# Two-layer graph kernel: the last Gaussian's square is moved ahead of the logarithm, a quarter of it to GpSimd, and four smaller edits beside it

## The reference

```python
# layer 0: four Gaussians of each adj element, normalised over the four, summed along the row
w  = exp(-0.5 * (adj[..., None] - mean) ** 2 / (1e-14 + prec ** 2))   # (8, 1024, 1024, 4)
ws = sum(w / sum(w, -1), axis=2)                                      # (8, 1024, 4)
h  = concat over k of ws[..., k] * (x @ W0[k].T)                      # (8, 1024, 512)
x1 = layernorm(x + h)
# layer 1: one of four experts for each batch, then batch norm over the batches of an expert
top1 = argmax(mean(x1, rows) @ router_w + router_b)
out  = adj @ (x1 @ expert_w[top1])
y    = relu(batchnorm_per_expert(out) * gamma + beta)
return layernorm(x1 + y)
```

## Time and profile before

| what | value |
|---|---|
| time, median of 3 runs | 885.05 us (884.5 to 885.08) |
| the profiled execution's own time | 887.86 us |
| its span | 886.1 us |
| busy share of the span PE / DVE / ACT / POOL | 85% / 85% / 87% / 78% |
| solo exponential of tile 0, tile 63 starts at | 16.9 us, 717.2 us |

### The profile page before, as it was taken

One profiled execution on the slowest core, in us unless ns is written; L12 is line 12 of the kernel. 1 busy time (PEld: TensorE's weight loads), 2 busy tenths in 40 slices (PEclk: granted clock), 3 DMA queues, 4 the chain that ended last, 5 costly groups with the idle time before them and its releaser, 6 DMA issues.

```text
span 886.1 us, 12505 instructions
## 1 busy us (share of the span) xinstructions
PE 753.0 (85%) x3922; PEld 349.8 (39%) x3922; DVE 755.4 (85%) x1643; ACT 766.9 (87%) x774; POOL 687.7 (78%) x772
## 2 busy tenths in 40 slices
PE   1444469799999999999999999999999999997661
PEld 1111124344444444444444444444444444445440
DVE  2999988699999999999999999999999992227994
ACT  6999998799999999999999999999999961116983
POOL 6699999988888888888888888888888622004794
PEclk9966679999999999999999999999999999998996
DMA  8799886977797779778977797779787728229999
GB/s 231 210 270 261 190 238 166 225 183 192 193 240 193 193 192 239 193 192 195 242 193 190 196 240 192 193 182 249 191 190 168 153 86 330 95 83 392 348 383 359
DMA packets 263925, 191.71 MB, mean 216 GB/s; under 512 B 210098, under 2 KB 210098, under 8 KB 262322
## 3 DMA queue, kind: packets, MB, share of 16 engines
q1 hardware_dynamic: 263714, 190.90, 79.7%
q10 hardware_dynamic: 144, 0.00, 0.0%
HBM read 91.78 MB, written 48.76 MB: 159 GB/s over the span
## 4 chain that ended last, share of the span: by engine, by line
ACT 35%; DVE 26%; POOL 19%; PE 12%; issue 4%; DMA 2%; SPq 0%; POOLq 0%; DVEq 0%; ACTq 0%
DVE ps_t L967 19%; ACT wgt L654 12%; PE ps_z L1136 6%; ACT ps_t L663 6%; ACT ps_t L665 5%; ACT adj_in L648 5%; ACT ps_t L659 5%; POOL adj_cut L512 3%; DVE x_in L951 3%; PE ps_o L1154 3%; DVE wgt L929 3%; POOL x_turn L523 2%; POOL adj_in L507 2%; PE ps_t L1154 2%; POOL adj_cut L510 2%
## 5 line engine op out<-in xcount | busy, mean ns | idle before, releaser
L1136 PE MATMUL ps_z<-adjT,x1p 128*128 128x512 f16 x1536 | 341.3, 379 | 0.0
L1122 PE MATMUL ps_h<-w0T,x_turn 128*128 128x512 f16 x768 | 194.4, 407 | 74.8 <-DVE x_in L951 65.0
L967 DVE TENSOR_TENSOR ps_t<-ps_t,wgt 128x1024 f32<-128x1024 f32 x192 | 234.9, 1224 | 19.0 <-ACT ps_t L659 17.8
L929 DVE SCALAR_TENSOR_TENSOR wgt<-wgt,ps_t 128x1024 f32<-128x1024 f32 x192 | 224.7, 1214 | 15.8 <-ACT ps_t L665 15.8
L1136 PEld LDWEIGHTS ps_z<-adjT,x1p 128*128 128x128 f16 x1536 | 150.2, 98 | 180.5
L648 ACT ACTIVATE wgt<-adj_in,neg_mu 128x1024 f32<-128x1024 f32 x192 | 205.6, 1134 | 7.5 <-POOL neg_mu L567 7.4
L654 ACT ACTIVATE wgt<-wgt 128x3072 f32<-128x3072 f32 x64 | 176.5, 2757 | 0.0
L1154 PE MATMUL ps_o<-zT,w_sel 128*128 128x512 f16 x696 | 161.2, 382 | 4.9 <-DMA w_sel<-w_planes 4.1
L1122 PEld LDWEIGHTS ps_h<-w0T,x_turn 128*128 128x128 f16 x768 | 74.9, 103 | 184.7 <-issue 107.1
L512 POOL TENSOR_TENSOR adj_cut<-adj_in,adj_cut 128x1024 f16<-128x1024 f32 x64 | 136.6, 2134 | 5.3
L1154 PEld LDWEIGHTS ps_o<-zT,w_sel 128*128 128x128 f16 x696 | 68.3, 98 | 88.2 <-DMA w_sel<-w_planes 4.6
(11 more groups left out here) (221 smaller groups left out, 778.2 us busy)
## 6 DMA issues: line engine op xcount, KB each, us to landing
adj_in<-in_adj_dram SPq DMA_DIRECT2D x64, 512.0 KB, 4.0
x_in<-in_x_dram SPq DMA_DIRECT2D x64, 256.0 KB, 4.3
x_spill<-x_in SPq DMA_DIRECT2D x28, 512.0 KB, 3.4
out_spill<-o_stage SPq DMA_DIRECT2D x50, 256.0 KB, 3.1
w_sel<-w_planes SPq DMA_DIRECT2D x8, 1024.0 KB, 8.0
adjT<-x_spill SPq DMA_DIRECT2D x6, 1024.0 KB, 10.2
out_dram<-adjT SPq DMA_DIRECT2D x5, 1024.0 KB, 7.8
adjT<-out_spill SPq DMA_DIRECT2D x4, 1024.0 KB, 12.5
```

Source lines behind the costliest of these rows:

```text
L929: v.scalar_tensor_tensor(out=wgt[:, m % 2, j, :], in0=wgt[:, m % 2, j, :], scalar=SUM_SCALE / W0_SCALE, in1=tot, op0=ALU.mult, op1=ALU.mul ...
L967: v.tensor_tensor(tot, tot, wgt[:, n % 2, j, :], ALU.add).then_inc(dve_tot, 1)
L1122: last = te.matmul(ps_h[:, n % 2, :], xT[:, n % 2, left, c, :], w0T[:, right, c, :], start=(c + i == 0), stop=(c == C - 1 and i == 2))
L1136: last = te.matmul(ps_z[:, u % 2, :], x1p[:, b % 2, left, t, k * P:(k + 1) * P], adjT[:, b % 2, right, t, half * HALF:(half + 1) * HALF], ...
```

## The change

What it does:

1. ACT's square for the solo Gaussian goes from its place behind the others' exponential to one ahead of the logarithm of the tile before (`square(n, SOLO, ...)` ahead of `sum_reciprocal(n - 1)`).
2. From tile 9 (`SQ_FROM`) ACT squares only columns 256 to 1023 of it. POOL does columns 0 to 255 with a multiply-add and a multiply, in place, after its two cuts; it waits for ACT's three other squares of that tile, and the solo exponential waits for POOL (`pool_sq`).
3. x is no longer multiplied by 16 (`X_SCALE`) ahead of its cut: one POOL instruction a tile less.
4. DVE makes its three adds onto `tot` one behind the other; `weighted` for kernels 2 and 3 comes behind them.
5. SP's fetch of a batch's expert weights is written one iteration earlier; its waits go with it (`dve_route`, `pe_o`).
6. In iteration 12 alone, where two z units are to be taken, the second is taken behind the others' exponential, and its low part one iteration later.

```diff
@@ sync, iteration n
-                if u % T == 0 and 0 <= u < TILES:
-                    m = u // T
+                if (u + 1) % T == 0 and 0 <= u + 1 < TILES:
+                    m = (u + 1) // T
...
                     sp.wait_ge(dve_route, m + 1)
-                    wait(sp, pe_o, u)
+                    wait(sp, pe_o, u + 1)
@@ gpsimd
-                g.tensor_scalar(tile, tile, X_SCALE, 1.0, ALU.mult, ALU.mult).then_inc(pool_xs, 1)
-                pool.wait_ge(pool_xs, m + 1)
...
+            def square(m):
+                cols = adj_in[:, m % ADJ_RING, 0:POOL_SQ]
+                pool.wait_ge(act_sq, NK * m + NK - 1)
+                g.tensor_scalar(cols, cols, spread_of[:, SOLO:SOLO + 1], neg_mu[:, SOLO:SOLO + 1],
+                                ALU.mult, ALU.add).then_inc(pool_line, 1)
+                pool.wait_ge(pool_line, m - SQ_FROM + 1)
+                g.tensor_tensor(cols, cols, cols, ALU.mult).then_inc(pool_sq, 1)
...
                     cut_x(n + 2)
+                if SQ_FROM <= n < TILES:
+                    square(n)
@@ scalar
                 act.wait_ge(act_sq, NK * n + NK)
+                wait(act, pool_sq, n - SQ_FROM + 1)
                 wait(act, dve_ws, NK * n - 1)
...
+                if n < TILES:
+                    act.wait_ge(pool_al, n + 1)
+                    if n == 0:
+                        load_spread(SOLO)
+                    first = POOL_SQ if n >= SQ_FROM else 0
+                    if first:
+                        act.wait_ge(act_sq, NK * n + NK - 1)
+                    square(n, SOLO, adj_in[:, n % ADJ_RING, first:NR], first)
                 if 0 <= n - 1 < TILES:
                     sum_reciprocal(n - 1)
                 if n < TILES:
                     weigh_others(n)
-                    act.wait_ge(pool_al, n + 1)
-                    if n == 0:
-                        load_spread(SOLO)
-                    square(n, SOLO, adj_in[:, n % ADJ_RING, :])
+                    take_z(z_halves(n - 1)[1])
                     weigh_solo(n)
@@ vector
                 weighted(n - 1, (0, 1))
-                sum_of_two(n, 0)
-                weighted(n - 1, (2,))
-                sum_of_two(n, 1)
-                weighted(n - 1, (3,))
-                sum_of_two(n, 2)
+                for j in range(NK - 1):
+                    sum_of_two(n, j)
+                weighted(n - 1, (2, 3))
```

More of the change, by code:

```diff
@@ L18 @@
 SUM_SCALE = 2.0 ** 60
-X_SCALE = 2.0 ** 4
 W0_SCALE = 2.0 ** 8
@@ L27 @@
 W_SCALE = 2.0 ** 8
+POOL_SQ = 256
+SQ_FROM = 9
 SOLO = 2
@@ L162, in gnn_program @@
         pool_as, pool_ah, pool_al = (sem(f"pool_{k}") for k in ("as", "ah", "al"))
-        pool_xs, pool_xh, pool_xl = (sem(f"pool_{k}") for k in ("xs", "xh", "xl"))
+        pool_xh, pool_xl = (sem(f"pool_{k}") for k in ("xh", "xl"))
+        pool_line, pool_sq = sem("pool_line"), sem("pool_sq")
         pool_neg, pool_x1, pool_1h, pool_1l = (sem(f"pool_{k}") for k in ("neg", "x1", "1h", "1l"))
@@ L278, in z_unit, with z_halves @@
             return range(n - Z_LAG, min(TILES, n - Z_LAG + 1))
+        def z_halves(n):
+            return z_unit(n)[:1], z_unit(n)[1:]
         def o_units(n):
@@ L452, in _ @@
                     sp.wait_ge(dve_route, m + 1)
-                    wait(sp, pe_o, u)
-                    if u == 0:
+                    wait(sp, pe_o, u + 1)
+                    if m == 0:
                         sp.wait_ge(planes_stored, 16 * E)
@@ L529, in norm_pair @@
                 pool.wait_ge(dve_mv, 2 * p + 2)
-                g.tensor_scalar(rstd[:, p % 2, :], y_mv[:, p % 2, :, 1], X1_SCALE ** -2, LN_EPS * (X_SCALE / X1_SCALE) ** 2,
+                g.tensor_scalar(rstd[:, p % 2, :], y_mv[:, p % 2, :, 1], X1_SCALE ** -2, LN_EPS / X1_SCALE ** 2,
                                 ALU.mult, ALU.add).then_inc(pool_var, 1)
@@ L645, in load_spread, with square @@
                 act.reg_load(spread[k], spread_of[0:1, k:k + 1].bitcast(I32))
-            def square(n, k, to):
-                s.activation(to, adj_in[:, n % ADJ_RING, :], ACT.Square, bias=neg_mu[:, k:k + 1],
+            def square(n, k, to, first=0):
+                s.activation(to, adj_in[:, n % ADJ_RING, first:NR], ACT.Square, bias=neg_mu[:, k:k + 1],
                              scale=spread[k]).then_inc(act_sq, 1)
@@ L665, in sum_reciprocal, with take_z @@
                 s.activation(tot, tot, ACT.Exp, scale=-1.0).then_inc(act_rec, 1)
-            def take_z(n):
-                for u in z_unit(n):
+            def take_z(units):
+                for u in units:
                     half, k = u % T // G, u % G
@@ L711, in _ @@
                 if z_taken_first(n - 1):
-                    take_z(n - 1)
+                    take_z(z_halves(n - 1)[0])
                 take_o(n - 1)
                 if not z_taken_first(n - 1):
-                    take_z(n - 1)
+                    take_z(z_halves(n - 1)[0])
+                if n < TILES:
[6 more added lines that the diff above has]
+                    square(n, SOLO, adj_in[:, n % ADJ_RING, first:NR], first)
                 if 0 <= n - 1 < TILES:
@@ L972, in _ @@
                 if n != FLUSH:
-                    for u in z_unit(n - 1):
+                    for u in (*z_halves(n - 2)[1], *z_halves(n - 1)[0]):
                         low_z(u)
```

## The result

The changed kernel took 923.62 us (median of 4 runs, 922.1 to 925.13) against 884.77 of before (884.14 to 885.08): ratio 1.0438, 95% interval 1.0424 to 1.0452. It is 38.9 us slower. Predicted were 921, range 908 to 931. The profiled executions differ by less, 923.64 against 887.86, 35.8 us: before's lay 2.8 above its own timed runs.

The account below looks back on a forecast made before the run. Bound: a dependency ring through `tot` between ACT and DVE, with ACT's own list within 0.1 us. Steady tiles +34.1, SP +1, end +1.4, tiles 1 to 14 -0.1: +36.4 on the median's 885.05, 921 us, range 908 to 931.

Parts of the forecast that it names:

- The ring over ACT: Steady tile, solo exponential to the next, through ACT's moved square, logarithm, reciprocal and DVE's row sums: 11.56 us.
- Three adds in a row: DVE's adds onto `tot`: path over them 0.24 us shorter, but worth nothing in the steady tiles.
- late weighted addition: DVE's `weighted` behind the three adds: releases PE's h at S + 5.56 (S: solo exponential's start), 1.4 us later.
- +0.5 every eighth tile: Iterations with z ahead of o: `take_o` needs PE's last product and is 0.48 ahead of `take_z`, +0.5 us.
- +1.4 at the end: After tile 62 PE alone is the path and starts from h(63), 1.4 us later in its beat.
- The second ring: Over two tiles, from late h through PE's h, o, z to `take_z` and the solo exponential: 23.18 us, 11.59 a tile.
- The 0.1 that I gave PE's signal to ACT: Between PE's z and ACT's `take_z`, in the two-tile path: a signal estimated at 0.1 us.
- Tiles 15 to 62: Steady stretch: 48 tiles each 0.71 us longer, +34.1, plus 1 us for SP's earlier fetch.
- the routing: Small instructions between DVE's row sums: about +0.15 us once in eight tiles, an estimate.
- the 5.3 stall: Iteration 13, where ACT waited 5.32 us: earlier-fetched weights are there before o, giving -5.3 in tile 14.
- Tiles 1 to 14: Start of the kernel: +5.5 in tiles 1 to 8, later gains and losses, in sum -0.1 us.
- The rival that took ACT's busy share as the bound: ACT's busy time sets the whole time; relieving it makes the kernel faster, 866 us; chance 0.07.

Follow-up runs that it names:

- where the ring was repaired: Changed kernel with the square back behind the others' exponential and the weighted additions back between the adds: 887.07 us, ratio 1.0027.
- the version with 128 columns: Changed kernel with square and weighted additions back, POOL squaring 128 columns instead of 256, early fetch for the first batch alone: 879.71 us, ratio 0.9945.
- the versions with an early h: Changed kernel with square and weighted additions back, early fetch for first batch alone; POOL with 128 columns 879.71 us, with none 882.3 us.
- the last run of the section above: Changed kernel with square and weighted additions back, early fetch for the first batch alone, no columns by POOL: 882.3 us, ratio 0.9977.

## Why the prediction was right

- **The ring over ACT.** Forecast 11.56, measured 11.57, with ACT's idle time and its releaser as said (0.98 against 1.1) and the 768-column square at 0.93. The run with the square put back shows that its place is the cause, the two runs with another share of POOL that its length counts column by column until POOL is late.
- **Three adds in a row, late weighted addition.** Forecast: nothing, +0.5 every eighth tile, +1.4 at the end. Measured: nothing, +0.48, +1.8. The run with the weighted additions back is 6.7 faster against 4.8 expected: 1.9 of it lie before tile 14, where h is late for the first z and o, which I had not counted. The second ring, over two tiles and PE, was put at 23.18; the changed kernel's tiles keep 2 x 11.57 = 23.14, so it did not bind there. It bound alone when the square was back. The 0.1 that I gave PE's signal to ACT came from no row; where ACT waits for z it starts 0.04 after the product's end (133.76 + 5.34 against 139.14).
- **Tiles 15 to 62.** Forecast 48 x 0.71 + 1 = 35.1; measured 33.99 - 0.95 = 33.0. The steady tiles followed the first ring (11.57) and not the second (11.59), the routing cost 0.13 (tiles of 11.70) where I had guessed 0.15, and nothing was lost to SP.
- **POOL.** Pair 1.26 against 1.25, hidden. Its work for two tiles was 21.8 and not 22.04. It was the bound with half of the columns, and nearly so where the ring was repaired.
- **Fetch.** That it holds back adj loads and that POOL's idle time hides this was right in the changed kernel; with the ring repaired POOL's waits for these loads make up most of the 0.11 a tile between 11.02 and the 10.91 of the version with 128 columns, though no run has the fetch alone put back there. That it takes away the 5.3 stall was the step that failed: the changed kernel without it is no slower. In its place the runs show a fetch that is early in either place (2.2 and 2.9 after the solo exponential of tile 12, instead of 8.0), and PE that is ready for it later (13.3 after it instead of 12.1). In the versions with an early h the early fetch is part of a start 5.2 to 6.5 shorter; it was not run by itself there.
- **Tiles 1 to 14.** Forecast -0.1, measured +0.95. Tiles 9 and 10 took 10.82 and not 10.61: with nothing between them, the in-place square waits for the third square ahead of it (`act_sq`), a step of 3.31 instead of 3.11 that I left out. Tile 11 took 12.04 and not 11.06; see below.
- **The size.** Between the profiled executions +35.8 against +36.4 forecast; between the medians +38.9. The 3 us between these two lie in the difference of before's profiled execution from its timed runs. No run shows where it comes from.

The rival that took ACT's busy share as the bound, which the Trainium skill ("Perfetto Trace Analysis", Identifying the Most-Contended Engine) would have led to, is refuted here: ACT fell from 99% to 91% of the stretch and the kernel lost 39 us. Relief in the old place helped by 0.08 a tile, all by which ACT's own list was later than the row sums.

## What to carry to other kernels

When two engines pass one buffer back and forth, find the ring and count what stands in it, not what the engines do in sum. Work that lies beside the other engine's part of the ring is free up to that part's length; the same work on the other side of the hand-over costs its whole length in every round, even if it got shorter on the way. And when a ring is shortened, others may lie close behind: here two tiles over PE and POOL's list were within 3%, and what waited behind a fetch lost its cover. Compute them all before giving an engine more work.

## What the runs showed of the hardware

**DVE and POOL blocked one another.** The instruction that makes an expert's low part on DVE reads two tiles in SBUF, one float32 and one float16; in the kernel before the eight of them took 1.19 to 2.15 each, 11.9 in sum. In the run with the square alone put back they took 1.19 to 3.15, 14.7 in sum. The longest, in iteration 3:

```profile
46.76 2.13 POOL L521 TENSOR_TENSOR adj_cut<-adj_in,adj_cut 128x1024 f16<-128x1024 f32 x1
46.82 3.15 DVE L1005 SCALAR_TENSOR_TENSOR x1p<-adjT,x1p 128x1024 f16<-128x1024 f32 x1
...
48.86 1.59 POOL L528 TENSOR_SCALAR x_turn<-x_in 128x512 f16<-128x512 f32 x1
```

DVE's instruction came 0.06 after POOL's and lasted till 1.1 after its end; POOL's next took 1.59 instead of 0.61. The solo exponential of tile 3 then waited 2.17 for the row sums. The Trainium skill ("SBUF — State Buffer", Who interferes with whom) has the port pair that DVE and GpSimd share as an exclusive lock, and says that a DVE instruction with two SBUF inputs contends with a GpSimd instruction that reads SBUF; the rows agree with that. Tiles 3, 6 and 8 of this run took 12.9, 12.1 and 12.1.

Who waits was decided by a tenth of a microsecond. In the last run of the section above, with no columns by POOL, the same two instructions met the other way round:

```profile
46.40 1.19 DVE L1005 SCALAR_TENSOR_TENSOR x1p<-adjT,x1p 128x1024 f16<-128x1024 f32 x1
46.55 3.04 POOL L521 TENSOR_TENSOR adj_cut<-adj_in,adj_cut 128x1024 f16<-128x1024 f32 x1
```

DVE came 0.15 first and took its 1.19; POOL's cut took 3.04 instead of 2.13, and tile 3 lost nothing (10.96). The version with 128 columns has the same program up to there, yet its POOL came 0.10 first (46.31 against 46.41), DVE took 3.11, and tile 3 took 12.49. So the two profiled executions differ by 1.8 us at tile 8 (109.11 and 107.29) by chance of order, and a difference of that size in the first tiles shows no effect of an edit. Whether POOL's shorter list makes the bad order more frequent is open.

**PE's clock after a wait.** In the changed kernel PE waited 5.54 us before h of tile 10; the product then took 5.05 instead of 2.75. The granted clock was 0.50 of full speed (1.2 GHz) from 130 to 133 us and 1.00 (2.4 GHz) from 134 on, 0.64 over this window:

```profile
130.00:135.00 5.00, 5.00 (x16) 1.93 (x15) 4.28 (x10) 4.01 (x3) 4.69 (x6) 0.64 0.56 105
```

The first z was late by it, and `take_z` in tile 11 waited 0.83 (at 139.14). The kernel before has the same slow product there (4.37 after a wait of 6.23), but its h starts 4.14 after the solo exponential of tile 9 and not 5.55, and its z is in time.
